# Feed-forward tile rebuilt: grid rounding through an integer Square in PSUM, new engines and orders for its steps

## The chip, the cores and the metric

The kernel runs on one core of a Trainium2 chip. The metric is the device time in microseconds (us) of one execution. Five queues run beside each other: TensorE (PE in the profile), VectorE (DVE), ScalarE (ACT), GpSimd (POOL) and SyncE (SP), which issues the transfers. They hand work to each other by counting semaphores.

## The reference

Input `x` is (16, 256, 256), `ctx` has the same shape. The first half is cross attention with 16 heads of 16; the second, which the change is about, is a feed-forward block whose three products are taken on blockwise FP4 values: each block of 16 values is scaled by its largest magnitude over 6, rounded to the grid 0, 0.5, 1, 1.5, 2, 3, 4, 6 with its sign, and scaled back.

```python
def fp4_quant_dequant(x):                 # BLOCK = 16
    scale = jnp.maximum(jnp.max(jnp.abs(xb), axis=-1, keepdims=True) / 6.0, 1e-12)
    xn = xb / scale
    q = _GRID[jnp.searchsorted(_MID, jnp.abs(xn))] * jnp.sign(xn) * scale
...
def _L0_ffn_ref(x, w_gate, w_up, w_down):   # 256 -> 704 -> 256
    gate = fp4_linear(x, w_gate)
    y = fp4_linear(x, w_up)
    h = jax.nn.silu(gate) * y
    return fp4_linear(h, w_down)
x = x + _L0_xattn_ref(_layernorm(x, axis=-1), ctx_1024, ctx_1024)
x = x + _L0_ffn_ref(_layernorm(x, axis=-1), w_gate, w_up, w_down)
```

## The kernel before

The attention runs first, as 16 pipelined steps of one batch each. Beside it the weights are rounded, a sixteenth a step. In the last full attention step (batch 15) TensorE transposes the rounded weights in 14 lots and VectorE copies each lot from PSUM to SBUF (`weights_out`). Then comes the feed-forward stage: 32 tiles of 128 rows. Nothing schedules it: each engine runs the function `ffn_step(st)` for step numbers that rise by one, and in step s an engine works on several tiles at once (`st.has(2)` guards the work on tile s+2, `st.has(-1)` that on tile s-1). An engine takes its instructions in the order in which they are written there.

A tile goes through these stages, with the lines of the program:

- normalise: statistics on VectorE (L709, L717, L722), the power -0.5 on GpSimd (L425), subtract and multiply on VectorE (L698);
- quantise x (256 wide, the program's XN and XC): block maxima (L704), limits and reciprocal (L607, L608, L612), multiply by the inverse on VectorE (L725), |z| times 2^22 on ScalarE (L516), max with a constant on VectorE (L731), add and subtract of that on GpSimd (L407, L409), multiply by the scale (L420);
- two transposes on TensorE into PSUM (L922) and a copy out on ScalarE (L511);
- four products of 352 columns (L909), gate and up, for the halves a = 0 and a = 1; Silu on ScalarE (L490), product with the up half on VectorE (L681), into HN;
- quantise h (704 wide): block maxima (L735), limits and reciprocal (L607, L608, L612), multiply (L738), three ScalarE statements (L521, L499, L501), add and subtract on GpSimd (L407, L409), multiply by the scale on VectorE (L753);
- six transposes (L933), copy out (L506), six products of 256 columns (L942), residual sum on VectorE (L689), store (L316).

Every buffer of the stage lies in the storage of the attention's `KS` and `QS`, so the profile shows XN, XC, HN, HC and the rest under those names. In PSUM, the products have banks of their own: gate halves in MX0 and SC0, up halves in PV and SC1. The x transposes lie in MX1, the result in SC2.

The rounding rests on adding a large number and subtracting it again, with a number that grows with |z|, so that the step of the fp32 sum is the step of the grid:

```python
def grid(z, c, sem_, wait_sem, st, off):          # GpSimd; c = max(|z| * 2^22 + ..., ...)
    nc.gpsimd.tensor_tensor(z, z, c, ALU.add).then_inc(sem_, 1)
    pool.wait_ge(sem_, st.times(off, 2, 1))
    nc.gpsimd.tensor_tensor(z, z, c, ALU.subtract).then_inc(sem_, 1)
```

Of the kernel before, what the change touches and what calls it, by code (L numbers as in the profile page):

```python
# [4 lines left out]
fp32 = mybir.dt.float32  # L5
bf16 = mybir.dt.bfloat16
ALU = mybir.AluOpType
# [5 lines left out]
QT = S // 128  # L13
# [12 lines left out]
MAGIC, ONE, UP, TINY = 2.0 ** 22, 1 + 2.0 ** -21, 1 + 2.0 ** -23, 1e-12  # L26
WCOLS = 3 * NT * D
# [4 lines left out]
CONSTS = 8  # L32
# [50 lines left out]
def ffn_steps(eng, body):  # L83
    steps(eng, body, 0, 5, (TILES - 8) // 2, 2, TILES + 3, TILES)


def program(nc, x, ctx_in, wg_in, wu_in, wd_in, out):
# [6 lines left out]
    with es:  # L94
# [17 lines left out]
        below = sb("below", [128, 1])  # L112
# [9 lines left out]
        KS = [sb(f"KS{r}", [128, H, S], bf16) for r in range(RING)]  # L122
        QS = [sb(f"QS{r}", [128, H, S], bf16) for r in range(RING)]
# [14 lines left out]
        fstats, fmv = sb("fstats", [128, 6]), [sb(f"fmv{r}", [128, 2]) for r in range(2)]  # L138
        fve = [sb(f"fve{r}", [128, 1]) for r in range(2)]
        frstd = [sb(f"frstd{r}", [128, 1]) for r in range(2)]  # L140
        xmax, xscale, xinv = ([sb(f"{n}{r}", [128, D // BLK]) for r in range(2)] for n in ("xmax", "xscale", "xinv"))
        hmax, hscale, hinv = ([sb(f"{n}{r}", [128, FI // BLK]) for r in range(2)] for n in ("hmax", "hscale", "hinv"))

        def carve(stack, *widths):

            words, at, carved = stack[:, :, :].rearrange("p h t -> p (h t)").bitcast(fp32), 0, []
            for w in widths:
                carved.append(words[:, at:at + w])
                at += w
            return carved  # L150

        WTR = [carve(z, 2 * FI)[0].rearrange("p (k c) -> p k c", k=2) for z in (KS[0], QS[0])]
        WDT = carve(KS[1], NT * D)[0].rearrange("p (k c) -> p k c", c=D)
        XN0, XN1, XC0, XC1, XQ0, XQ1, XT0, XT1 = carve(QS[1], *[D] * 8)
        XN = [XN0, XN1]
        XC = [XC0, XC1]
        XQ = [XQ0, XQ1]
        XT = [z.rearrange("p (k c) -> p k c", k=2) for z in (XT0, XT1)]
        (HN0, HC0, SG0), (HN1, HC1, SG1) = (carve(z, FI, FI, FH) for z in (KS[2], QS[2]))
        HN = [HN0, HN1]  # L160
        HC = [HC0, HC1]
        SG = [SG0, SG1]
        (HQ0, HQ1, OB0), (HT0, HT1, OB1) = (carve(z, NT * 128, NT * 128, D) for z in (KS[3], QS[3]))
        HQ = [HQ0, HQ1]
        HT = [z.rearrange("p (k c) -> p k c", k=NT) for z in (HT0, HT1)]
        OB = [OB0, OB1]

        SC = [pb(f"SC{r}", [128, QT, S]) for r in range(3)]
        MX = [pb(f"MX{r}", [128, QT, S]) for r in range(2)]
# [34 lines left out]
        h_abs, x_abs = sem("h_abs"), sem("x_abs")  # L204
        f_seq, fve_ready, frstd_ready = sem("f_seq"), sem("fve_ready"), sem("frstd_ready")
        x_seq, xc_ready, x_pool, xq_ready = sem("x_seq"), sem("xc_ready"), sem("x_pool"), sem("xq_ready")
        xp_ready, xt_ready, gu_ready, silu_done, h_done = (sem(n) for n in
            ("xp_ready", "xt_ready", "gu_ready", "silu_done", "h_done"))
        h_seq, hc_ready, h_pool, hq_ready = sem("h_seq"), sem("hc_ready"), sem("h_pool"), sem("hq_ready")
        hp_ready, ht_ready, down_ready, out_ready = (sem(n) for n in ("hp_ready", "ht_ready", "down_ready", "out_ready"))  # L210
# [29 lines left out]
        for m in range(2):  # L240
            for k in range(2):
                for a in range(2):
                    rs = range(3 * a, 3 * a + 3)
                    lots.append((WTR[m][:, k, 384 * a:min(FI, 384 * a + 384)],
                                 [WN[m][0:min(128, FI - 128 * r), r, 128 * k:128 * (k + 1)] for r in rs]))
        for c in range(NT):
            lots.append((WDT[:, c, :], [WD[:, r, 128 * c:128 * (c + 1)] for r in range(2)]))
# [9 lines left out]
        def _(sp):  # L257
# [62 lines left out]

            for t in (-3, -2):
                ffn_step(Step(t, TILES, 2))
            attention_step(Step(B - 1, B, RING))
            ffn_step(Step(-1, TILES, 2))
# [6 lines left out]
        def _(pool):  # L331
# [13 lines left out]
            nc.gpsimd.memset(below[:, :], -MAGIC * ONE).then_inc(consts, 1)  # L345

# [57 lines left out]
            def grid(z, c, sem_, wait_sem, st, off):  # L404

                pool.wait_ge(wait_sem, st.times(off, 1, 1))
                nc.gpsimd.tensor_tensor(z, z, c, ALU.add).then_inc(sem_, 1)  # L407
                pool.wait_ge(sem_, st.times(off, 2, 1))
                nc.gpsimd.tensor_tensor(z, z, c, ALU.subtract).then_inc(sem_, 1)  # L409

# [18 lines left out]
            for t in (-3, -2):  # L429
                ffn_step(Step(t, TILES, 2))  # L430
# [546 lines left out]
```

## Time and profile before

| | |
|---|---|
| time, median of 3 runs (lowest to highest) | 636.11 us (634.38 to 636.55) |
| the profiled execution: its time, its span | 636.03 us, 634.2 us |
| TensorE busy | 561.2 us, 88% of the span |
| VectorE busy | 515.0 us, 81% |
| ScalarE busy | 355.3 us, 56% |
| GpSimd busy | 324.4 us, 51% |
| attention with the weights | up to about 306 us of the span |
| first feed-forward product, last residual sum | 314.04 us, 631.55 us |

The span is that of the instructions; the rest of an execution's time, 1.8 us here, lies around it. Busy time is the union of an engine's instructions. The chain that ended last puts 41% of the span on TensorE and 25% on GpSimd, but it joins two stages that differ; the feed-forward stage has to be read by itself. The granted clock of TensorE over the span is 0.989 of full speed.

### The profile page before, as it was taken

The numbers are of one execution on the slowest core, as the hardware profiler recorded it, in microseconds if no ns is written. First come the engines' busy times: TensorE is split into PE (matmuls) and PEld (weight loads), VectorE is DVE, ScalarE is ACT, GpSimd is POOL, SyncE is SP. The second block draws the span as 40 slices with busy tenths as digits, with TensorE's granted clock in tenths as the row PEclk, the third lists the DMA queues.
The fourth block names the chain that finished last, engine by engine and source line by source line (L and its number), as shares of the span: only waits on it lengthen the run. The fifth ranks groups of instructions, "written<-read, shape, count | busy, mean of one in ns | idle before, by whom it ended". The sixth has DMA issues, their size and how long they took to land.

```text
span 634.2 us, 12943 instructions
## 1 busy us (share of the span) xinstructions
PE 561.2 (88%) x3561; PEld 341.6 (54%) x3588; DVE 515.0 (81%) x1171; ACT 355.3 (56%) x656; POOL 324.4 (51%) x386
## 2 busy tenths in 40 slices
PE   2489999999999999998679999999999999999996
PEld 1135555555555555545446665665665665665664
DVE  1498888889888888875478989889889889889863
ACT  2226877778877778776434445445345354354341
POOL 3243344444444444322356676776766766766740
PEclk9999999999999999999898999999999999999997
DMA  7834444444444443300000000000000000000000
GB/s 228 194 101 135 133 138 127 126 127 125 125 125 133 133 133 100 100 4 3 0 1 9 9 18 17 8 17 17 8 17 17 8 17 17 8 17 14 11 18 25
DMA packets 43796, 40.59 MB, mean 64 GB/s; under 512 B 4728, under 2 KB 43512, under 8 KB 43768
## 3 DMA queue, kind: packets, MB, share of 16 engines
q1 hardware_dynamic: 43768, 40.26, 22.4%
q8 instruction: 13, 0.21, 0.1%
q14 instruction: 15, 0.12, 0.1%
HBM read 10.55 MB, written 4.19 MB: 23 GB/s over the span
## 4 chain that ended last, share of the span: by engine, by line
PE 41%; POOL 25%; issue 15%; DVE 8%; ACT 5%; DMA 2%; SPq 2%; POOLq 1%; another core or an unknown queue 0%; ACTq 0%; DVEq 0%
PE PV L862 11%; PE SC L830 10%; PE MX L844 8%; POOL QS L409 6%; POOL QS L407 6%; POOL frstd L425 4%; POOL KS L409 4%; POOL KS L407 3%; PE T L772 3%; PE T L816 2%; PE SC L942 2%; ACT KP L448 2%; PE T L779 2%; POOL QS L420 2%; ACT P L457 1%
## 5 line engine op out<-in xcount | busy, mean ns | idle before, releaser
L544 DVE TENSOR_REDUCE MF<-MX 128x2 f32<-128x512 f32 x256 | 170.1, 686 | 32.8 <-PE MX L844 30.4
L457 ACT ACTIVATE P<-SC 128x512 f32<-128x512 f32 x256 | 147.2, 599 | 47.6 <-PE SC L830 45.7
L844 PE MATMUL MX<-KS,QS 96*128 96x256 bf16 x512 | 104.8, 289 | 6.9 <-DMA QS<-QP 3.4
L942 PE MATMUL SC<-KS,QS 128*128 128x256 f32 x384 | 93.8, 395 | 17.2 <-ACT QS L506 17.2
L830 PE MATMUL SC<-QS,KS 98*128 98x256 bf16 x512 | 99.7, 278 | 1.1 <-ACT P L457 0.7
L942 PEld LDWEIGHTS SC<-KS,QS 128*128 128x128 f32 x384 | 72.0, 194 | 42.6 <-ACT QS L506 33.7
L862 PE MATMUL PV<-P,VA 128*32 128x256 f32 x1024 | 81.6, 391 | 3.6
L407 POOL TENSOR_TENSOR QS<-QS 128x256 f32<-128x256 f32 (+1 forms) x47 | 48.3, 1027 | 63.9 <-ACT QS L501 35.8
L830 PEld LDWEIGHTS SC<-QS,KS 98*128 98x128 bf16 x512 | 39.2, 98 | 58.8 <-ACT P L457 31.9
L844 PEld LDWEIGHTS MX<-KS,QS 96*128 96x128 bf16 x512 | 47.6, 101 | 28.8 <-DVE MF L544 18.4
L409 POOL TENSOR_TENSOR QS<-QS 128x256 f32<-128x256 f32 (+1 forms) x47 | 49.8, 1059 | 3.7
L725 DVE TENSOR_TENSOR QS<-QS,xinv 128x256 f32<-128x256 f32 x32 | 51.2, 1600 | 0.0
L521 ACT ACTIVATE QS<-QS 128x704 f32<-128x704 f32 x16 | 12.7, 791 | 65.9 <-DVE QS L738 65.9
L521 ACT ACTIVATE KS<-KS 128x704 f32<-128x704 f32 x16 | 12.7, 791 | 64.7 <-DVE KS L738 64.7
L407 POOL TENSOR_TENSOR KS<-KS 128x704 f32<-128x704 f32 x16 | 26.9, 1680 | 40.9 <-ACT KS L501 40.9
L391 POOL TENSOR_TENSOR W<-W,WC 128x288 f32<-128x288 f32 (+1 forms) x16 | 12.7, 791 | 67.3 <-DVE WC L635 67.3
L909 PE MATMUL MX<-KS,QS 128*128 128x352 f32 x128 | 44.4, 470 | 1.0 <-ACT QS L511 1.0
L909 PE MATMUL SC<-KS,QS 128*128 128x352 f32 x128 | 44.4, 470 | 0.0
L909 PE MATMUL PV<-QS 128*128 128x352 f32 x128 | 43.2, 460 | 0.0
L909 PE MATMUL SC<-QS 128*128 128x352 f32 x128 | 43.2, 460 | 0.0
L425 POOL TENSOR_TENSOR frstd<-fve,mhalf 128x1 f32<-128x1 f32 x32 | 35.7, 1116 | 7.6 <-DVE fve L722 7.6
L448 ACT ACTIVATE KP<-T 128x512 bf16<-128x512 f32 x48 | 28.6, 596 | 18.4 <-PE T L772 12.2
(107 smaller groups left out, 993.4 us busy)
## 6 DMA issues: line engine op xcount, KB each, us to landing
KS<-KP SPq DMA_DIRECT2D x96, 128.0 KB, 2.4
QS<-QP SPq DMA_DIRECT2D x96, 128.0 KB, 2.4
X<-in_x SPq DMA_DIRECT2D x16, 256.0 KB, 2.9
C<-in_ctx SPq DMA_DIRECT2D x16, 256.0 KB, 3.1
out<-KS SPq DMA_DIRECT2D x16, 128.0 KB, 1.7
out<-QS SPq DMA_DIRECT2D x16, 128.0 KB, 1.7
W<-in_L_ffn_w_down SPq DMA_DIRECT2D x1, 704.0 KB, 8.3
W<-in_L_ffn_w_gate SPq DMA_DIRECT2D x1, 640.0 KB, 5.1
```

Source lines behind the costliest of these rows:

```text
L407: nc.gpsimd.tensor_tensor(z, z, c, ALU.add).then_inc(sem_, 1)
L409: nc.gpsimd.tensor_tensor(z, z, c, ALU.subtract).then_inc(sem_, 1)
L425: nc.gpsimd.tensor_tensor(frstd[r][:, :], fve[r][:, :], mhalf[:, 0:1], ALU.pow).then_inc(frstd_ready, 1)
L448: nc.scalar.activation(parts[:, n, :], bank, ACT.Copy).then_inc(out_sem, 1)
L457: nc.scalar.activation(P[g % 2][:, j, :, :], SC[h % 3][:, :, :], ACT.Exp, scale=0.25).then_inc(exp_done, 1)
L544: nc.vector.tensor_reduce(MF[st.slot(off, 2)][:, :, h:h + 1], MX[h % 2][:, :, :], AX.X, ALU.max, negate=True).then_inc(mx_done, 1)
L725: nc.vector.tensor_tensor(blocks(XN[r][:, :]), blocks(XN[r][:, :]), each(xinv[r][:, :]), ALU.mult).then_inc(x_seq, 1)
L830: last = nc.tensor.matmul(SC[h % 3][:, k, :], KS[r][0:ROWS, h, k * 128:(k + 1) * 128], QS[r][0:ROWS, h, :], start=True, stop=True)
L844: last = nc.tensor.matmul(MX[h % 2][:, q, :], QS[r][0:PROD, h, q * 128:(q + 1) * 128], KS[r][0:PROD, h, :], start=True, stop=True)
L862: last = nc.tensor.matmul(PV[32 * j:32 * (j + 1), g % 2, :], VA[r][:, k, HG * g + j, :], P[g % 2][:, j, k, :], start=(k == 0), stop=(k == ...
L909: last = nc.tensor.matmul((GP, UPP)[m][a], XT[st.slot(0, 2)][:, k, :], WTR[m][:, k, a * FH:(a + 1) * FH], start=(k == 0), stop=(k == 1))
L942: last = nc.tensor.matmul(DP, HT[r][:, c, :], WDT[:, c, :], start=(c == 0), stop=(c == NT - 1))
```

## The change

The steps of a feed-forward tile are redistributed and reordered. What stays: the tiles, the products with their sizes and operand types, the attention.

1. The grid. ScalarE squares the scaled z and writes the square as an integer into PSUM (one statement each for x and h); VectorE then adds the square, a constant and z, and in a second statement takes the square and constant minus z, which leaves the rounded value with its sign turned (the scales are negative now). ScalarE's Abs, Relu and Copy of h, its Abs of x, VectorE's max for x and GpSimd's four add and subtract statements go.
2. No VectorE statement reads two tensors from SBUF. The multiplications by the inverses and by the h scale, which had two SBUF inputs on VectorE (L725, L738, L753), are on GpSimd; normalising is one ScalarE Identity with a bias and a scale; the block maxima and the statistics lie in PSUM, so the limits read PSUM.
3. PSUM: one gate bank G and one up bank U serve both halves, so each product waits for the reader of the one before.
4. The order of each engine's work in a step; x is prepared one tile further ahead (`st.has(4)`); two steps instead of one and two of the ramp stand before the last attention step, and two behind it.
5. `weights_out` is on ScalarE.
6. `XN`, `XQ`, `OB` and `SG` have SBUF of their own; h buffers and weights lie in `KS` and `QS` still, at other places. GpSimd's power is taken over two columns.

```diff
-        GP = [MX[0][:, :, :].rearrange("p q s -> p (q s)")[:, 0:FH], SC[0][:, :, :].rearrange("p q s -> p (q s)")[:, 0:FH]]
-        UPP = [PV[:, :, :].rearrange("p q s -> p (q s)")[:, 0:FH], SC[1][:, :, :].rearrange("p q s -> p (q s)")[:, 0:FH]]
-        DP = SC[2][:, 0, :]
-        XP = MX[1][:, 0, :].rearrange("p (k c) -> p k c", k=2)
+        G = bank(SC[0])[:, 0:FH]
+        U = bank(SC[1])[:, 0:FH]
+        hmax = bank(SC[1])[:, FH:FH + FI // BLK]
+        XP = bank(SC[2])[:, 0:D]
+        DP = PV[:, 0, :]
+        fmv, xmax = PV[:, 1, 0:2], PV[:, 1, 16:16 + D // BLK]
+        SQ = MXB[:, :, :, :].rearrange("p r q s -> p (r q s)").bitcast(int32)
+        HSQ, XSQ = SQ[:, 0:FI], SQ[:, FI:FI + D]
...
@@ GpSimd, ffn_step
-                if st.has(-1) and st.first < TILES:
-                    grid(HN[r][:, :], HC[r][:, :], h_pool, hc_ready, st, -1)
-                if st.has(2):
-                    grid(XN[r][:, :], XC[r][:, :], x_pool, xc_ready, st, 2)
...
+                if st.has(-1):
+                    pool.wait_ge(h_inv, st.times(-1, 1, 1))
+                    nc.gpsimd.tensor_tensor(blocks(HN[r][:, :]), blocks(HN[r][:, :]), each(hinv[r][:, :]),
+                                            ALU.mult).then_inc(hm_ready, 1)
+                if st.has(4):
+                    nc.gpsimd.tensor_tensor(frstd[r][:, :], fve[r][:, :], mhalf[:, :], ALU.pow).then_inc(frstd_ready, 1)
+                if st.has(-1):
+                    pool.wait_ge(h_grid, st.times(-1, 1, 1))
+                    nc.gpsimd.tensor_tensor(blocks(HQ[r][:, 0:FI]), blocks(HN[r][:, :]), each(hscale[r][:, :]),
+                                            ALU.mult).then_inc(hq_ready, 1)
...
@@ ScalarE, ffn_step
+                if st.has(3):
+                    nc.scalar.activation(XN[r][:, :], tile(st.item(3)), ACT.Identity, bias=fbias[r][:, 0:1],
+                                         scale=frstd[r][:, 0:1]).then_inc(xn_ready, 1)
                 if st.has(0):
                     silu(st, 0)
+                if st.has(-1):
+                    act.wait_ge(hm_ready, st.times(-1, 1, 1))
+                    if st.has(1):
+                        act.wait_ge(x_grid, st.times(1, 1, 1))
+                    nc.scalar.activation(HSQ, HN[r][:, :], ACT.Square, scale=CURVE).then_inc(hsq_ready, 1)
...
@@ VectorE
+            def round_up(z, square, done):
+                nc.vector.scalar_tensor_tensor(z, square, BASE, z, ALU.add, ALU.add).then_inc(done, 1)
+
+            def round_back(z, square, done):
+                nc.vector.scalar_tensor_tensor(z, square, BASE, z, ALU.add, ALU.subtract).then_inc(done, 1)
...
@@ TensorE, inner(st, a, m) and the down product
+                    pe.wait_ge(silu_done, st.times(0, 2, a))
+                elif a == 0:
+                    pe.wait_ge(h_lim, st.times(-1, 2, 2))
+                else:
+                    pe.wait_ge(h_done, st.times(0, 2, 1))
...
+                    product(DP, HH[r], WDH, NT).then_inc(down_ready, 1)
```

On TensorE, the two steps of the loop stood like this; T is the PSUM of the h transposes, the rows of L909 are the gate and up products, L922 the x transposes, L942 the down product.

```order
L909 MATMUL MX<-KS,QS 128x352 x2
L909 MATMUL PV<-QS 128x352 x2
L919 REGISTER_ALU
L922 MATMUL MX<-ident,QS 128x128 x2
L907 REGISTER_ALU
L909 MATMUL SC<-KS,QS 128x352 x2
L928 REGISTER_ALU
L931 REGISTER_ALU
L933 MATMUL T<-ident,KS 128x128 x6
L909 MATMUL SC<-QS 128x352 x2
L942 MATMUL SC<-KS,QS 128x256 x6
```

The same step of the changed kernel; L934 holds all products, L953 both kinds of transposes.

```order
L953 MATMUL T<-ident,HQ 128x128 x6
L942 REGISTER_ALU
L943 ISA
L934 MATMUL SC<-WH,XH 128x352 x2
L971 REGISTER_ALU
L953 MATMUL SC<-ident,XQ 128x128 x2
L934 MATMUL SC<-WH,XH 128x352 x2
L943 REGISTER_ALU
L934 MATMUL SC<-WH,XH 128x352 x4
L988 REGISTER_ALU
L934 MATMUL PV<-WDH,HH 128x256 x6
```

The number and size of the matmuls are the same; the h transposes moved from between the second half's two products to the head of the step, and the x transposes one product forward.

On VectorE, the second part of a step, from the up product's multiplication (L681) on:

```order
L725 TENSOR_TENSOR QS<-QS,xinv 128x256
L681 TENSOR_TENSOR KS<-SC,QS 128x352
L731 TENSOR_SCALAR QS<-QS 128x256
L735 TENSOR_REDUCE hmax<-KS 128x44
L607 TENSOR_SCALAR hscale<-hmax 128x44
L608 TENSOR_SCALAR hinv<-hmax 128x44
L612 RECIPROCAL hinv<-hinv 128x44
L738 TENSOR_TENSOR KS<-KS,hinv 128x704
L753 TENSOR_TENSOR KS<-QS,hscale 128x704
```

And of the changed kernel, from the first half's multiplication (L702) to the end of the step:

```order
L702 TENSOR_TENSOR HN<-SC,SG 128x352
L718 SCALAR_TENSOR_TENSOR HN<-MX,HN 128x704
L762 RECIPROCAL xinv<-xinv 128x16
L721 SCALAR_TENSOR_TENSOR HN<-MX,HN 128x704
L702 TENSOR_TENSOR HN<-SC,SG 128x352
L770 TENSOR_REDUCE SC<-HN 128x44
L718 SCALAR_TENSOR_TENSOR XN<-MX,XN 128x256
L721 SCALAR_TENSOR_TENSOR XN<-MX,XN 128x256
L714 TENSOR_SCALAR hscale<-SC 128x44
L715 TENSOR_SCALAR hinv<-SC 128x44
L783 RECIPROCAL hinv<-hinv 128x44
```

The two rounding statements of the previous tile's h now stand between the two halves of this tile, the two of x stand between the h maxima and the h limits, and the multiplications with block values are gone from the engine.

## Rows read from the trace of the kernel before

**Rows 1.** Busy time by engine, from the page.
```profile
PE 561.2 (88%) x3561; PEld 341.6 (54%) x3588; DVE 515.0 (81%) x1171; ACT 355.3 (56%) x656; POOL 324.4 (51%) x386
```

**Rows 2.** Stretches of the feed-forward stage: length, busy PE, PEld, DVE, ACT, POOL, granted clock.
```profile
310.00:360.00 50.00, 40.41 (x151) 27.20 (x152) 37.38 (x89) 18.67 (x36) 32.21 (x34) 0.93 0.02 6
360.00:410.00 50.00, 46.17 (x187) 30.11 (x186) 45.20 (x100) 22.22 (x40) 34.92 (x34) 1.00 0.04 14
```

**Rows 3.** Timeline, TensorE, one tile: start, length, what, idle before it.
```profile
449.98 0.88 PE L933 MATMUL T<-ident,KS 128*128 128x128 f32 x6
450.69 1.35 PE L909 MATMUL SC<-QS 128*128 128x352 f32 x4
452.63 2.86 PE L942 MATMUL SC<-KS,QS 128*128 128x256 f32 x12 [0.60 <-ACT QS L506]
455.33 1.35 PE L909 MATMUL MX<-KS,QS 128*128 128x352 f32 x4
456.51 1.35 PE L909 MATMUL PV<-QS 128*128 128x352 f32 x4
458.05 0.44 PE L922 MATMUL MX<-ident,QS 128*128 128x128 f32 x2 [0.19 <-POOL QS L420]
458.32 1.35 PE L909 MATMUL SC<-KS,QS 128*128 128x352 f32 x4
459.68 0.87 PE L933 MATMUL T<-ident,KS 128*128 128x128 f32 x6
```

**Rows 4.** Timeline of the same tile, the other engines.
```profile
451.96 1.67 POOL L407 TENSOR_TENSOR QS<-QS 128x704 f32<-128x704 f32 x1 [2.44 <-ACT QS L501]
452.08 1.84 DVE L725 TENSOR_TENSOR QS<-QS,xinv 128x256 f32<-128x256 f32 x1
453.71 1.75 POOL L409 TENSOR_TENSOR QS<-QS 128x704 f32<-128x704 f32 x1
453.95 0.42 ACT L516 ACTIVATE QS<-QS 128x256 f32<-128x256 f32 x1 [1.09 <-DVE QS L725]
454.75 0.53 DVE L681 TENSOR_TENSOR KS<-SC,QS 128x352 f32<-128x352 f32 x1 [0.83 <-ACT QS L490]
455.54 0.87 DVE L735 TENSOR_REDUCE hmax<-KS 128x44 f32<-128x704 f32 x1
456.54 0.72 DVE L608 TENSOR_SCALAR hinv<-hmax 128x44 f32<-128x44 f32 x1
457.75 0.99 DVE L738 TENSOR_TENSOR KS<-KS,hinv 128x704 f32<-128x704 f32 x1
458.77 0.79 ACT L521 ACTIVATE KS<-KS 128x704 f32<-128x704 f32 x1 [4.06 <-DVE KS L738]
461.58 1.67 POOL L407 TENSOR_TENSOR KS<-KS 128x704 f32<-128x704 f32 x1 [2.44 <-ACT KS L501]
```

**Rows 5.** Timeline, ramp: end of the attention, first product.
```profile
292.68 0.42 ACT L516 ACTIVATE QS<-QS 128x256 f32<-128x256 f32 x1 [2.51 <-DVE QS L725]
...
314.04 2.56 PE L909 MATMUL MX<-KS,QS 128*128 128x352 f32 x4
```

**Rows 6.** Timeline of the last tiles.
```profile
596.14 0.42 DVE L725 TENSOR_TENSOR QS<-QS,xinv 128x256 f32<-128x256 f32 x1
...
609.27 1.35 PE L909 MATMUL MX<-KS,QS 128*128 128x352 f32 x4
609.29 0.17 DVE L608 TENSOR_SCALAR hinv<-hmax 128x44 f32<-128x44 f32 x1
...
621.29 5.49 PE L942 MATMUL SC<-KS,QS 128*128 128x256 f32 x12 [0.90 <-ACT QS L506]
...
631.55 0.42 DVE L689 TENSOR_TENSOR QS<-SC,X 128x256 f32<-128x256 f32 x1 [4.31 <-PE SC L942]
```

**Rows 7.** GpSimd groups by shape: busy us, mean ns, idle before.
```profile
L407 POOL TENSOR_TENSOR QS<-QS 128x256 f32<-128x256 f32 x32 | 23.2, 726 | 28.1 <-DVE QS L731 28.1
L397 POOL TENSOR_TENSOR W<-W,wscale 128x288 f32<-128x288 f32 x8 | 5.4, 676 | 1.4 <-POOL W L394 1.4
```

More of the change, by code:

```diff
@@ L344, in _ @@
                                         base=0, pattern=[[-1, 128]], channel_multiplier=1).then_inc(consts, 1)
-            nc.gpsimd.memset(below[:, :], -MAGIC * ONE).then_inc(consts, 1)
+            for r in range(2):
+                nc.gpsimd.memset(fve[r][:, :], 1.0).then_inc(consts, 1)
             nc.gpsimd.memset(mhalf[:, :], -0.5).then_inc(consts, 1)
@@ L489, in silu @@
                 act.wait_ge(h_done, st.times(-1, 2, a + 1))
-                nc.scalar.activation(SG[a][:, :], GP[a], ACT.Silu).then_inc(silu_done, 1)
+                nc.scalar.activation(SG[a][:, :], G, ACT.Silu).then_inc(silu_done, 1)
             def ffn_step(st):
-                if st.has(0):
-                    silu(st, 0)
-                if st.has(-1) and st.first < TILES:
-                    r = st.slot(-1, 2)
-                    act.wait_ge(h_abs, st.times(-1, 2, 1))
-                    nc.scalar.activation(HC[r][:, :], HC[r][:, :], ACT.Relu, bias=below[:, :]).then_inc(h_abs, 1)
-                    act.wait_ge(h_abs, st.times(-1, 2, 2))
-                    nc.scalar.activation(HC[r][:, :], HC[r][:, :], ACT.Copy, bias=MAGIC * ONE).then_inc(hc_ready, 1)
                 if st.has(-2):
@@ L612, in invert @@
                 nc.vector.reciprocal(inv, inv).then_inc(sem_, 1)
-            def scales(amax, scale, inv, sem_, per, first, st, off):
-                limits(amax, scale, inv, sem_, per, first, st, off)
-                invert(inv, sem_, per, first, st, off)
-                dve.wait_ge(sem_, st.times(off, per, first + 3))
             def weight_maxima(st):
@@ new lines, in round_up @@
+            def round_up(z, square, done):
+                nc.vector.scalar_tensor_tensor(z, square, BASE, z, ALU.add, ALU.add).then_inc(done, 1)
+            def round_back(z, square, done):
+                nc.vector.scalar_tensor_tensor(z, square, BASE, z, ALU.add, ALU.subtract).then_inc(done, 1)
+            def ffn_step(st):
+                mean_var, amax = (fmv0[:, :], xmax0[:, :]) if st.first < 0 else (fmv, xmax)
+                if st.first == 0:
+                    dve.wait_ge(pv_out, 2 * B)
+                if st.has(4):
+                    dve.wait_ge(x1_ready, st.times(4, 1, 1))
+                    gate(dve)
+                    nc.vector.bn_stats(fstats[:, :], tile(st.item(4))).then_inc(f_stats, 1)
@@ L749, in ffn_step @@
[L749 to L754 removed]
+                    dve.wait_ge(h_max, st.times(0, 1, 1))
+                    block_limits(hmax, hscale[r][:, :], hinv[r][:, :], h_lim)
@@ L900, in attention_step, with product @@
                             values(st, g, 1)
+            def product(dst, x, w, count):
+                for c in range(count):
+                    last = nc.tensor.matmul(dst, x[:, c, :], w[:, c, :], start=(c == 0), stop=(c == count - 1))
+                return last
             def inner(st, a, m):
+                r = st.slot(0, 2)
                 if m == 0:
@@ L930, in ffn_step @@
                         pe.wait_ge(zeroed, 2)
+                        pe.wait_ge(o_norm, QT * B)
                     pe.wait_ge(ht_ready, st.times(-2, 1))
                     for c in range(NT):
-                        last = nc.tensor.transpose(HP[:, c, :], HQ[r][:, 128 * c:128 * (c + 1)], ident[:, :])
+                        last = turn(HP[:, c, :], HQ[r][:, 128 * c:128 * (c + 1)], c % 4 == 0)
                     last.then_inc(hp_ready, 1)
+                if st.has(0):
+                    inner(st, 0, 0)
+                if st.has(1):
+                    r = st.slot(1, 2)
+                    pe.wait_ge(xq_ready, st.times(1, 1, 1))
+                    pe.wait_ge(xt_ready, st.times(1, 1))
+                    if st.first == -1:
+                        pe.wait_ge(exp_done, B * H)
+                    for k in range(2):
+                        last = turn(XP[:, 128 * k:128 * (k + 1)], XQ[r][:, 128 * k:128 * (k + 1)], k == 0)
+                    last.then_inc(xp_ready, 1)
+                if st.has(0):
+                    inner(st, 0, 1)
+                    inner(st, 1, 0)
                 if st.has(0):
@@ L940, in ffn_step @@
                     pe.wait_ge(out_ready, st.times(-2, 1))
-                    for c in range(NT):
-                        last = nc.tensor.matmul(DP, HT[r][:, c, :], WDT[:, c, :], start=(c == 0), stop=(c == NT - 1))
-                    last.then_inc(down_ready, 1)
+                    if st.has(4):
+                        pe.wait_ge(fneg_ready, st.times(4, 1, 1))
+                    elif st.has(3):
+                        pe.wait_ge(x_lim, st.times(3, 2, 2))
+                    product(DP, HH[r], WDH, NT).then_inc(down_ready, 1)
             pe.wait_ge(consts, CONSTS)
```

289 lines of the change are left out of this document (146 added, 143 removed).

## The prediction

> **What bounds the kernel now.** The page's busy times come first [rows 1]: TensorE 88% and VectorE 81% of the span, no other engine above 56%. These are means over two unlike stages, and the change touches only the second, so the next view is that of stretches. From 360 to 410 us, a steady piece of the feed-forward stage, TensorE is busy 46.2 of 50 us and VectorE 45.2 [rows 2]. Both look nearly full, and the question is which of them sets the pace.
>
> The timeline of one tile answers it. TensorE first [rows 3]. I take what a group costs as the distance to the start of the next group where that did not wait: six h transposes 0.71 us (449.98 to 450.69), four products of the gate and up kind 1.18 each (455.33 to 456.51), the down product 2.70 (452.63 to 455.33), two x transposes 0.27. The sum is 0.71 + 4.72 + 2.70 + 0.27 = 8.40 us. But the tile takes 9.62 us: GpSimd's L407 starts at 451.96 and again, one tile on, at 461.58 [rows 4]. So TensorE loses 1.2 us a tile, part as idle time before the down product (0.60, for ScalarE's copy) and before the x transposes (0.19), the rest where a group has to drain before the next may start.
>
> The other engines show the ring that sets 9.62 [rows 4]. GpSimd's L407 starts at 451.96. VectorE's L725, a multiplication with two inputs in SBUF, starts at 452.08 and takes 1.84 us; at 596.14, with no GpSimd statement beside its start, the same statement takes 0.42 [rows 6]. It ends 0.29 us after GpSimd's L407 does: it was held. Behind it come ScalarE's L516 (453.95), a Silu, the second up half (L681, 454.75), the h maxima (L735, 455.54), the limits, of which L608 takes 0.72 here and 0.17 at 609.29 [rows 4, 6], the multiplication L738 (457.75 to 458.74), and three ScalarE statements from 458.77 on, which release GpSimd's next L407. The two holds add 1.42 + 0.55 = 2.0 us to VectorE's tile. L681 (one input in PSUM) took 0.53 us although GpSimd's L409 ran beside it from 453.71 to 455.46 [rows 4], so such a statement is not held.
>
> **The change, part by part.** The sum is made against the profiled execution, 636.03 us; the median of the runs, 636.11, is the same within 0.1.
>
> TensorE keeps its groups, so 8.40 us a tile is its floor. The reordering puts h transposes, whose input is a whole step old, directly behind the down product, and the x transposes between two products; nothing then has to drain. The single gate and up banks add waits: the second gate product waits for the first Silu, which has 1.45 us for it (the up product and x transposes between, 1.18 + 0.27) and needs about 0.5 for the 352 elements that L681 takes 0.53 for; the second up product waits for VectorE's first half, 0.53 us [rows 4], behind a gate product of 1.18. Both fit. If a queue is late there, up to 0.4 us a tile comes back. I take 8.45 us a tile.
>
> VectorE's new list per tile, by the nearest rows: rounding of h twice. The operation, two tensors and a constant with the square in PSUM, has no row. Its lower bound is one pass at the pace of the maxima, 0.87 for 704 elements; its upper bound twice that, 1.74. I take 0.89, because L681 with a PSUM and an SBUF input costs 0.53 for 352, and the statement reads no more than that does. Rounding of x twice at 0.42 each, two halves 1.06, h maxima 0.87, x maxima, statistics and residual sum at 0.42 each, limits and reciprocals together about 1.3 with the small ones: some 7.5 us, below 8.45. The list before was longer by the three block multiplications and the holds.
>
> GpSimd: two block multiplications of 704. L397 costs 676 ns for 288 against 726 ns for a plain 256 [rows 7]. Plain 704 costs 1.67 [rows 4], so the slope is (1.67 - 0.73)/448 = 2.1 ns per element; with it, 704 costs 0.68 + 416 x 2.1 ns = 1.55, with L397's own mean per element 1.65, and if its fixed part is like the plain one's, 1.4. I take 1.5. With two of 256 for x (0.6 each) and the power this is about 5.3 us a tile, not the bound; and GpSimd's four add and subtract statements go. ScalarE goes down to seven statements, the two largest 0.79 like L521 [rows 4], some 3.6 us: cover for each is an engine idle more than half of the tile. A write of integers to PSUM has no row; between nothing and twice 0.79 it adds at most 0.8 to the ring below.
>
> The new ring runs through h: second half 0.53, h maxima 0.87, the two x roundings that stand behind them 0.84, limits and reciprocal 0.79 (455.54 + 0.87 to 457.75, less the hold of 0.55), GpSimd 1.5, Square 0.79, the two h roundings 1.78, and then the next tile's second half, which stands behind them in VectorE's queue. With nine handovers at 0.03 to 0.05 (L725 to L516 took 0.03) that is 7.1 + 0.4 = 7.5 us. TensorE sets the pace with 0.9 us to spare.
>
> Stage by stage. From the first product of tile 0 (314.04) to that of tile 31 (609.27) the kernel now takes 295.2 us [rows 5, 6]. After: 31 x 8.45 = 262, plus 2 for half clock in the ramp (0.93 granted from 310 to 360 us is some 7 us at 1.2 instead of 2.4 GHz [rows 2]; before, other waits hid part of that), so 264: a gain of 31.2. The two first tiles lack transposes and down products, and wait for their chain instead; I let these cancel. Tail: now 631.97 - 609.27 = 22.7. After: four products 4.9, then 0.53 + 0.87 + 0.79 + 1.5 + 0.79 + 1.78, GpSimd 1.5, transposes 0.88, copy 0.79, down product 2.86, residual 0.42, handovers 0.4, together 18.0; the idle gaps let the clock fall as now, where the down product took 5.49 instead of 2.86 [rows 6, 3], so plus 3: 21.0, a gain of 1.7.
>
> The passage from attention costs nothing net in my sum. The wait of ScalarE for VectorE inside the last attention step, 2.5 us at 292.68 [rows 5], goes, and a shorter one for the first tile's bias comes. Against it, ScalarE gets 14 weight copies, about 0.42 each by its 256-wide statement [rows 4], 5.9 us beside the exponentials of one step; TensorE's next lot and VectorE wait for them. And the last batch's evacuation now stands behind the preparation of tiles 1 and 2 on ScalarE, with GpSimd's sums of the last two batches queued behind three feed-forward multiplications. The first product would come at 314 again, give or take 3.
>
> 636.0 - 31.2 - 1.7 = 603.1; I forecast 603.
>
> **Rivals.** First, the ring through h takes over: handovers or GpSimd's multiplications dearer than taken, or the square slower into PSUM. With 1.0 to 1.5 us more the tile takes 8.6 to 9.0, and the time is 603 + 31 x (0.15 to 0.55) = 608 to 620. For it: the ring has seven steps on three engines, of which three have no row. Against it: 0.9 us of slack. Chance 0.24.
>
> Second, slower than before: the rounding statements run at half pace, 1.74 and 0.84. That adds 2.6 to the ring, 7.5 + 2.6 = 10.1, and to VectorE's list, 10.1 as well; the starts that overlap take back 0.3. 31 x (9.8 - 8.45) = 42, so about 645. It decides from a rounding cost of 1.7 us for 704 elements on, where the tile takes the present 9.5. Against it: L681 and its full pace [rows 4]. Chance 0.06.
>
> The Trainium skill ("Vector Engine (DVE) Microarchitecture Reference", "Points that are easy to get wrong") says that a scalar_tensor_tensor with two SBUF sources wider than bf16 halves its throughput. One of the two lies in PSUM here, so by the letter of the rule the sum stays; if it held here nevertheless, it would be this rival. No row of this trace shows the operation.
>
> Third, the change does not do what it says: VectorE is still held by GpSimd, by 1.4 us a tile or more, and the tile stays at 9.5: 636. L681 speaks against it. Chance 0.02. Mishaps of the ramp make up the rest.
>
> **How the numbers follow.** TensorE's pace as forecast 0.67 (598 to 608); the h ring 0.24 (608 to 620); slower 0.06; no change 0.03. The range takes in the first case and most of the second: 596, the ramp 3 us better and no clock lost in the tail, to 617. A difference under 0.3%, 2 us, is about what a measurement of this kernel can't tell from none. Faster 0.91, same 0.03, slower 0.06.
>
> **What would show it.** Right: distance between equal TensorE groups 8.4 to 8.5 us; TensorE busy all of a steady stretch; L718 and L721 at 0.9 for 704 elements; no VectorE statement stretched beside GpSimd; idle time on VectorE before the first half. Wrong: idle time on TensorE before L934 put down to VectorE; L718 at 1.7; a first product later than 317 us.

## The result and the profile after

The changed kernel takes 593.13 us (median of 4, 591.61 to 593.94) where the kernel before took 635.25 in the runs beside it: 0.933 of it, with a 95% interval of 0.9305 to 0.9362. The forecast was 603 us with a range of 596 to 617. The direction, the mechanism and the new bound were forecast; the gain was put at 33 us and is 42, and the time lies outside the range.

From the page of the changed kernel: busy time by engine, and how the chain of work that ended last divides over the engines.

```profile
PE 541.5 (92%) x3561; PEld 346.9 (59%) x3588; DVE 447.8 (76%) x1154; ACT 329.9 (56%) x640; POOL 269.6 (46%) x389
PE 80%; issue 5%; ACT 5%; DVE 3%; POOL 2%; DMA 2%; SPq 2%; another core or an unknown queue 0%; POOLq 0%; ACTq 0%; DVEq 0%
```

Stretches of the same stage as in [rows 2] (length, busy PE, PEld, DVE, ACT, POOL, granted clock):

```profile
310.00:360.00 50.00, 44.87 (x189) 30.72 (x182) 36.24 (x113) 20.57 (x41) 28.13 (x40) 0.91 0.03 9
360.00:410.00 50.00, 50.00 (x220) 37.09 (x220) 41.04 (x117) 21.20 (x43) 28.56 (x36) 1.00 0.05 16
```

TensorE is busy for all 50 us of the steady stretch, where it had 46.17, and VectorE went from 45.20 to 41.04. TensorE's timeline for one tile, to be held against [rows 3]:

```profile
445.60 0.82 PE L953 MATMUL T<-ident,HQ 128*128 128x128 f32 x6
446.25 1.35 PE L934 MATMUL SC<-WH,XH 128*128 128x352 f32 x4
447.44 0.38 PE L953 MATMUL SC<-ident,XQ 128*128 128x128 f32 x2
447.66 3.72 PE L934 MATMUL SC<-WH,XH 128*128 128x352 f32 x12
451.21 2.75 PE L934 MATMUL PV<-WDH,HH 128*128 128x256 f32 x12
453.80 0.82 PE L953 MATMUL T<-ident,HQ 128*128 128x128 f32 x6
```

No group waited. From start to start: h transposes 0.65, gate product 1.19, x transposes 0.22, three products 3.55, down product 2.59, together 8.20 us a tile instead of 9.62. That is 0.25 under the 8.45 of the forecast, and 0.2 under what the forecast called TensorE's floor. The other engines from a tile's first half (L702) on, to be held against [rows 4]; L422 ends this tile's rounding, L411 and L535 begin the next one's:

```profile
441.04 0.53 DVE L702 TENSOR_TENSOR HN<-SC,SG 128x352 f32<-128x352 f32 x1 [0.29 <-PE SC L934]
441.48 0.88 DVE L718 SCALAR_TENSOR_TENSOR HN<-MX,HN 128x704 f32<-128x704 int32 x1
442.43 0.85 DVE L721 SCALAR_TENSOR_TENSOR HN<-MX,HN 128x704 f32<-128x704 int32 x1
443.44 1.39 POOL L422 TENSOR_TENSOR HQ<-HN,hscale 128x704 f32<-128x704 f32 x1 [2.13 <-DVE HN L721]
446.42 1.39 POOL L411 TENSOR_TENSOR HN<-HN,hinv 128x704 f32<-128x704 f32 x1
448.08 0.76 ACT L535 ACTIVATE MX<-HN 128x704 int32<-128x704 f32 x1
```

The operations that had no row cost what the forecast took or less: the rounding statements 0.88 and 0.85 us (0.89 taken), the Square into PSUM 0.76 (0.79), GpSimd's block multiplication 1.39 (1.5). VectorE now waits for TensorE before the first half (0.29).

Ramp and tail, TensorE's and VectorE's rows that answer to [rows 5, 6]:

```profile
309.18 0.66 PE L953 MATMUL SC<-ident,XQ 128*128 128x128 f32 x2 [3.59 <-POOL XQ L433]
309.77 1.94 PE L892 MATMUL PV<-P,VA 128*32 128x256 f32 x16
315.39 2.55 PE L934 MATMUL SC<-WH,XH 128*128 128x352 f32 x4
...
569.28 4.90 PE L934 MATMUL SC<-WH,XH 128*128 128x352 f32 x16
...
584.07 4.54 PE L934 MATMUL PV<-WDH,HH 128*128 128x256 f32 x12 [0.90 <-ACT HH L520]
588.65 0.42 DVE L710 TENSOR_TENSOR OB<-PV,X 128x256 f32<-128x256 f32 x1 [7.00 <-PE PV L934]
```

They divide the gain of the spans, 634.2 - 591.3 = 42.9 us, into the parts of the forecast:

| part | before | after | gain | forecast gain |
|---|---|---|---|---|
| to tile 0's first product | 314.0 | 315.4 | -1.4 | 0 |
| from there to tile 31's first product | 295.2 | 253.9 | 41.3 | 31.2 |
| from there to the end of the last residual sum | 22.7 | 19.8 | 2.9 | 1.7 |

### The profile page after: what moved, and what is told of

Same layout as the page of the kernel before. It is cut to its first block, busy times and chain, and to the rows that moved or that the text cites. A ratio compares the mean times of both kernels' runs of the same rounds, so it can differ in the third digit from the quotient of the medians.

```text
span 591.3 us, 12747 instructions
## 1 busy us (share of the span) xinstructions
PE 541.5 (92%) x3561; PEld 346.9 (59%) x3588; DVE 447.8 (76%) x1154; ACT 329.9 (56%) x640; POOL 269.6 (46%) x389
## 4 chain that ended last, share of the span: by engine, by line
PE 80%; issue 5%; ACT 5%; DVE 3%; POOL 2%; DMA 2%; SPq 2%; another core or an unknown queue 0%; POOLq 0%; ACTq 0%; DVEq 0%
PE SC L934 24%; PE PV L934 13%; PE PV L892 12%; PE SC L860 10%; PE MX L874 9%; PE T L953 4%; PE T L802 3%; PE T L846 3%; ACT P L473 2%; ACT KP L464 2%; PE T L809 2%; DVE MF L576 2%; PE SC L953 1%; DMA QS<-QP 1%; SPq L274 1%
## 5 line engine op out<-in xcount | busy, mean ns | idle before, releaser
L934 PE MATMUL SC<-WH,XH 128*128 128x352 f32 x512 | 163.2, 463 | 0.0
L934 PEld LDWEIGHTS SC<-WH,XH 128*128 128x128 f32 x512 | 93.2, 192 | 41.4 <-DVE HN L702 3.6
L874 PE MATMUL MX<-KS,QS 96*128 96x256 bf16 x512 | 104.4, 288 | 8.6 <-DMA QS<-QP 4.2
L934 PE MATMUL PV<-WDH,HH 128*128 128x256 f32 x384 | 90.0, 385 | 1.8 <-ACT HH L520 1.8
L934 PEld LDWEIGHTS PV<-WDH,HH 128*128 128x128 f32 x384 | 74.0, 193 | 17.2 <-ACT HH L520 2.3
L422 POOL TENSOR_TENSOR HQ<-HN,hscale 128x704 f32<-128x704 f32 x32 | 44.4, 1387 | 77.0 <-DVE HN L721 77.0
L520 ACT ACTIVATE HH<-T 128x768 f32<-128x768 f32 x32 | 25.9, 810 | 92.7 <-PE T L953 92.7
L874 PEld LDWEIGHTS MX<-KS,QS 96*128 96x128 bf16 x512 | 47.4, 100 | 30.4 <-DVE MF L576 18.6
L513 ACT ACTIVATE SG<-SC 128x352 f32<-128x352 f32 x64 | 29.4, 459 | 41.5 <-PE SC L934 41.5
L702 DVE TENSOR_TENSOR HN<-SC,SG 128x352 f32<-128x352 f32 x64 | 33.6, 525 | 22.5 <-PE SC L934 20.8
L411 POOL TENSOR_TENSOR HN<-HN,hinv 128x704 f32<-128x704 f32 x32 | 44.4, 1386 | 2.1 <-DVE hinv L783 2.0
L464 ACT ACTIVATE QP<-T 128x512 bf16<-128x512 f32 x48 | 29.2, 608 | 14.7 <-PE T L809 8.3
```

Of the source, the lines that this page charges most:

```text
L411: nc.gpsimd.tensor_tensor(blocks(HN[r][:, :]), blocks(HN[r][:, :]), each(hinv[r][:, :]), ALU.mult).then_inc(hm_ready, 1)
L422: nc.gpsimd.tensor_tensor(blocks(HQ[r][:, 0:FI]), blocks(HN[r][:, :]), each(hscale[r][:, :]), ALU.mult).then_inc(hq_ready, 1)
L464: nc.scalar.activation(parts[:, n, :], bank, ACT.Copy).then_inc(out_sem, 1)
L513: nc.scalar.activation(SG[a][:, :], G, ACT.Silu).then_inc(silu_done, 1)
L702: nc.vector.tensor_tensor(HN[st.slot(0, 2)][:, a * FH:(a + 1) * FH], U, SG[a][:, :], ALU.mult).then_inc(h_done, 1)
L874: last = nc.tensor.matmul(MX[h % 2][:, q, :], QS[r][0:PROD, h, q * 128:(q + 1) * 128], KS[r][0:PROD, h, :], start=True, stop=True)
```

## The experiments

The theory at this point, called A: TensorE alone sets the tile's 8.20 us; the ring through h needs 7.3 to 7.5; a statement of VectorE with two SBUF inputs is held by one of GpSimd that is running; and the 0.2 us a tile by which TensorE's floor was read too high is what a group costs more when it had to wait and could not load its first weights ahead. Its rivals: the ring is close behind TensorE (B), the hold has another cause, or TensorE's groups got cheaper by their new buffers. Most kernels here ran once; their times are compared with the 593.1 of the changed kernel and the 635.9 to 636.4 of the kernel before in the same sets of runs, and most verdicts rest on rows.

Two parts of a run move by themselves, and a single time has to be read with that in mind. The first is the start: early products of the attention wait for a transfer (L874; L875 in the kernel with the extra statement). In the changed kernel, in the one with the extra PSUM statement and in the one with the weight copies on VectorE:

```profile
27.43 0.61 PE L874 MATMUL MX<-KS,QS 96*128 96x256 bf16 x2 [4.21 <-DMA QS<-QP]
29.10 0.61 PE L875 MATMUL MX<-KS,QS 96*128 96x256 bf16 x2 [5.42 <-DMA QS<-QP]
30.09 0.61 PE L874 MATMUL MX<-KS,QS 96*128 96x256 bf16 x2 [5.65 <-DMA QS<-QP]
```

No edit touches this stretch, and it differs by up to 2.7 us. The second is the last down product: 4.54 us in the trace of the changed kernel, 2.86 in that of the kernel with the weight copies on VectorE, whose tail is the same. That is 1.7 us of granted clock which no edit there explains.

**Less work on TensorE.** One and three of the six down products left out:

```diff
-                    product(DP, HH[r], WDH, NT).then_inc(down_ready, 1)
+                    product(DP, HH[r], WDH, 5).then_inc(down_ready, 1)
```

(3 in the second kernel.)

> The changed kernel with one of the six products of each down projection left out (the result lacks that part of the sum). Theory A, TensorE alone sets the tile's 8.20 us and the ring through h needs about 7.4: one product pair costs 2.59/6 = 0.43 us, so the tile takes 7.77 and the time falls by 31 x 0.43 = 13 us to about 580. Theory B, the ring through h (VectorE's roundings, GpSimd, Square) is within 0.2 us of TensorE: the tile stays at 8.0 or more and the time at 587 or more.

> The changed kernel with three of the six products of each down projection left out. TensorE alone would need 8.20 - 1.30 = 6.90 us a tile and the time would be about 553. Theory A, with the ring through h at 7.3 to 7.5 us: the tile takes that, VectorE has no idle time ahead of the first half and GpSimd's multiplication releases Square late; time 565 to 571. Theory B: 8.0 or more, 587.

Measured: 579.5 us with five, 13.6 less, so the product pair (31 x 0.43 = 13.3) comes through whole. With three, 573.0: far from 553, but also 2.0 us above A's 565 to 571, of which the later start (28.72 against 27.43) explains 1.3. Steady rows with three:

```profile
443.52 1.39 POOL L422 TENSOR_TENSOR HQ<-HN,hscale 128x704 f32<-128x704 f32 x1 [2.16 <-DVE HN L721]
445.04 0.87 PE L953 MATMUL T<-ident,HQ 128*128 128x128 f32 x6 [0.46 <-POOL HQ L422]
441.56 0.88 DVE L718 SCALAR_TENSOR_TENSOR HN<-MX,HN 128x704 f32<-128x704 int32 x1
449.17 0.88 DVE L718 SCALAR_TENSOR_TENSOR HN<-MX,HN 128x704 f32<-128x704 int32 x1
```

The tile takes 7.61 us (441.56 to 449.17), a little over A's 7.3 to 7.5, and TensorE waits 0.46 us for GpSimd's HQ. So B is out: there were 0.6 us of slack behind TensorE. But the next ring is not the one that I had written down. As I read the rows, it runs rounding, GpSimd's multiplication by the scale, h transposes, the tile's first two products with the x transposes between them, and VectorE's first half, which stands ahead of the next rounding.

**One more statement on VectorE**, once with an input in PSUM, once with both in SBUF, ahead of the h maxima:

```diff
+                    nc.vector.tensor_tensor(C[0][:, 0, :], U[:, 0:D], HN[r][:, D:2 * D], ALU.add)
```

```diff
+                    nc.vector.tensor_tensor(C[0][:, 0, :], HN[r][:, 0:D], HN[r][:, D:2 * D], ALU.add)
```

> The changed kernel with one more VectorE statement per tile, 256 elements, one input in PSUM and one in SBUF, just before the h maxima, while GpSimd's multiplication by the h scale runs. Both theories: 0.42 us on VectorE, not held. Theory A (0.8 us of slack in the ring): time unchanged within 1 us. Theory B: 0.2 to 0.4 us a tile more, 6 to 12 us.

> The same extra statement with both inputs in SBUF. If a VectorE statement with two SBUF inputs is held by a GpSimd statement that runs, it starts at about 443.8 beside GpSimd's 1.39 us statement and takes 1.2 to 1.4 us instead of 0.42; the ring then needs 8.2 to 8.6 us and the time rises by 0 to 12 us. If the hold seen before had another cause (the block inverse read 16 times over, for one), it takes 0.42 and the time is that of the run with one PSUM input.

Measured: 595.1 and 601.1 us. The first is 2 us over the changed kernel where A allowed 1; 1.7 of them lie in the start (29.10 against 27.43), and the tile stays at 8.20 us. In the second the tile takes 8.44 us on average (316.35 to 578.12 for 31). Rows of the kernel with the PSUM input, then of the one with two SBUF inputs:

```profile
445.38 1.39 POOL L422 TENSOR_TENSOR HQ<-HN,hscale 128x704 f32<-128x704 f32 x1 [2.13 <-DVE HN L721]
445.79 0.42 DVE L770 TENSOR_TENSOR C<-SC,HN 128x256 f32<-128x256 f32 x1
```

```profile
439.92 1.39 POOL L422 TENSOR_TENSOR HQ<-HN,hscale 128x704 f32<-128x704 f32 x1 [1.90 <-DVE HN L721]
440.27 1.32 DVE L770 TENSOR_TENSOR C<-HN 128x256 f32<-128x256 f32 x1
441.26 0.81 POOL L427 TENSOR_TENSOR XN<-XN,xinv 128x256 f32<-128x256 f32 x1
```

The same work at the same place takes 0.42 us or 1.32, and in the second case it ends at 441.59, 0.28 after GpSimd's statement does at 441.31; the hold of L725 before looked the same. GpSimd's next statement in turn takes 0.81 us instead of 0.62. The statement reads nothing 16 times over, so that is not the cause. The Trainium skill ("SBUF — State Buffer", "SBUF: two separate sides") describes this as a pair of SBUF ports that the two engines share, which a VectorE statement with two SBUF inputs and a GpSimd statement cannot hold together and which whoever starts first keeps; the rows agree.

**The h multiplication by the inverse on VectorE again**, the statement of before with its two SBUF inputs:

```diff
-                    nc.gpsimd.tensor_tensor(blocks(HN[r][:, :]), blocks(HN[r][:, :]), each(hinv[r][:, :]),
-                                            ALU.mult).then_inc(hm_ready, 1)
...
+                    dve.wait_ge(h_inv, st.times(0, 1, 1))
+                    nc.vector.tensor_tensor(blocks(HN[r][:, :]), blocks(HN[r][:, :]), each(hinv[r][:, :]),
+                                            ALU.mult).then_inc(hm_ready, 1)
```

> The changed kernel with the h multiplication by the inverse on VectorE again (704 elements, two inputs in SBUF) instead of GpSimd. Theory A: VectorE's 7.3 us busy of 8.2 become 8.2 to 8.5 with the hold by GpSimd's statement for x that runs just then, so VectorE takes over from TensorE: 8.3 to 8.7 us a tile, time 596 to 609, and the statement takes 1.0 to 1.3 us. Rival: where the multiplication stands does not matter, because the order and the rounding made the gain: 8.2 us, 592 to 595.

Measured: 592.7 us. My expectation failed, in its price as in its sum:

```profile
445.81 0.89 DVE L780 TENSOR_TENSOR HN<-HN,hinv 128x704 f32<-128x704 f32 x1
445.83 0.92 POOL L434 TENSOR_TENSOR fbias<-fneg,frstd 128x1 f32<-128x1 f32 x1
360.00:410.00 50.00, 50.00 (x221) 37.17 (x220) 46.09 (x122) 21.48 (x43) 24.91 (x30) 1.00 0.05 16
```

VectorE started 0.02 us ahead of GpSimd, so GpSimd was held: its one-column product took 0.92 us instead of the 0.19 of the changed kernel. VectorE is busy 46.1 of 50 us and TensorE all of them. That no VectorE statement has two SBUF inputs is therefore no condition of the gain; only what else runs when one starts matters. The kernel before had this hold in both directions too: its one-column power (L425) takes 1.20 us in the steady tiles, where VectorE's L738 has started just before it, and 0.55 at 311.37, where no such statement runs.

**All three block multiplications on VectorE**, as before the change (the edit above, and the same for the h scale behind L721 and for x behind that):

> The changed kernel with all three block multiplications that the kernel before had on VectorE there again: h by its inverse, h by its scale, x by its inverse. Theory A: VectorE, busy 46.1 of 50 us with the first of them back, gets 0.89 + 0.42 us more a tile and becomes the bound: 8.9 us of work and what GpSimd's x statement and the ring add, 8.9 to 9.4 us a tile, time 615 to 631. Rival: what the change gained is the order and the rounding; with TensorE still the bound 8.2 to 8.4, 593 to 600.

Measured: 617.2 us. Two rows of VectorE, one tile apart:

```profile
439.90 0.52 DVE L686 TENSOR_TENSOR HN<-SC,SG 128x352 f32<-128x352 f32 x1
449.04 0.52 DVE L686 TENSOR_TENSOR HN<-SC,SG 128x352 f32<-128x352 f32 x1
```

9.14 us a tile, in the middle of what A gave. With the rest of the change in place, moving the three multiplications is worth 24 of the 42 us by the times, and 26 of the 41 by the stretch between the first products of tiles 0 and 31 (280.2 us here, 253.9 in the changed kernel). The other 15 to 18 come from the rest taken together (rounding and orders), which was not divided further. Since the first of the three costs nothing on VectorE by itself, this is no sum of three separate parts.

**The down product without its wait, in the kernel before:**

```diff
-                    pe.wait_ge(ht_ready, st.times(-2, 1, 1))
...
-                        last = nc.tensor.matmul(DP, HT[r][:, c, :], WDT[:, c, :], start=(c == 0), stop=(c == NT - 1))
+                        last = nc.tensor.matmul(DP, WDT[:, c, 0:128], WDT[:, c, :], start=(c == 0), stop=(c == NT - 1))
```

> The kernel before, with the down product's stationary operand read from a fixed slice of the weights, so that TensorE waits for no copy ahead of that group (the result is not the block's). Theory A: TensorE was not in the ring that set 9.62 us, so the idle 0.60 us ahead of the group goes elsewhere and the tile stays at 9.62, time 634 to 637; and a group whose first weights can be loaded while the group before still runs costs less from start to start than the 2.70 us read from a group that had waited: 2.59, with the start record 0.1 us behind the weight load. Rival: TensorE was in the ring and the tile falls by 0.3 to 0.6 us, time 618 to 627; or the group keeps 2.70, and the lower cost in the changed kernel comes from its banks and buffers.

Measured: 631.7 us. Rows of TensorE and GpSimd:

```profile
439.18 1.20 POOL L425 TENSOR_TENSOR frstd<-fve,mhalf 128x1 f32<-128x1 f32 x1
442.50 2.64 PEld L941 LDWEIGHTS SC<-KS 128*128 128x128 f32 x12
442.79 2.75 PE L941 MATMUL SC<-KS 128*128 128x256 f32 x12
445.38 1.35 PE L909 MATMUL MX<-KS,QS 128*128 128x352 f32 x4
448.81 1.20 POOL L425 TENSOR_TENSOR frstd<-fve,mhalf 128x1 f32<-128x1 f32 x1
```

The tile stays at 9.63 us (439.18 to 448.81): TensorE was not in the ring of before. And the group costs 2.59 (442.79 to 445.38) in the old banks and buffers, as in the changed kernel; its weight load starts 0.29 us ahead of its first matmul, where the load and matmul of the waiting group start together. The 4 us that it is faster lie in the last tiles, where the wait for the copy was exposed. 2.7 of them are clock: the down product that took 5.49 us takes 2.76 there. Whether the edit did that is not shown, as the clock of such a group differs between kernels with the same tail, too.

**The h transposes back in their old place** on TensorE, between the two products of the second half, with ScalarE's copy behind that of x:

> The changed kernel with the h transposes back between the two products of the second half on TensorE, and their copy on ScalarE behind that of the x transposes. Theory A: TensorE lost time before only where it really waited, and here nothing waits there: HQ is old, the copy ends 0.3 us before the down product: 8.20 us a tile, 592 to 595. Rival: the place of the transposes is what took the drains away: 0.3 to 0.6 us a tile more, 602 to 612.

Measured: 594.3 us, within A's 592 to 595, but not by A's 8.20 us a tile:

```profile
436.07 2.85 PE L934 MATMUL PV<-WDH,HH 128*128 128x256 f32 x12
...
443.46 0.81 ACT L540 ACTIVATE HH<-T 128x768 f32<-128x768 f32 x1 [1.54 <-PE T L953]
444.39 2.46 PEld L934 LDWEIGHTS PV<-WDH,HH 128*128 128x128 f32 x12 [0.43 <-issue]
444.40 2.85 PE L934 MATMUL PV<-WDH,HH 128*128 128x256 f32 x12
447.09 1.35 PE L934 MATMUL SC<-WH,XH 128*128 128x352 f32 x4
```

The tile takes 8.33 us (436.07 to 444.40). The copy ends at 444.27, 0.13 us before the down product starts, so TensorE shows no idle time. Yet its weight load starts only with the group, not 0.29 us ahead, and the group costs 2.69 again. An operand that is just in time was too late here for the early weight load. The place of the transposes is no matter of 0.3 to 0.6 us a tile, as the rival had it, but of 0.13. The time hides part of that, because the last down product ran at full clock (2.86 us).

**The weight copies on VectorE again:**

> The changed kernel with the 14 weight copies of the last attention step on VectorE again. Theory A: the copies were no bound on either engine: TensorE's last attention scores come at 304 to 305 as before, the first product within 1 us of 315.4, time 592 to 594. Rival: on ScalarE they delayed the exponentials and with them the end of the attention, so the first product comes 1 to 3 us sooner here, time 590 to 592.

Measured: 594.6 us, and the first product comes at 317.94 instead of 315.39, so neither expectation holds as it stands. But the whole delay lies in the start: it is there at 30.09 against 27.43. From there to TensorE's last attention products ahead of the passage it is 277.6 us (to 307.66), in the changed kernel 277.5 (to 304.95). So it makes no difference to the attention which engine copies the weights, as A had it.

**The order of the passage.** The last batch's final step ahead of ramp step -1, on every engine; and in a second kernel ahead of both ramp steps:

```diff
             attention_step(Step(B - 1, B, RING))
-            for t in (-2, -1):
-                ffn_step(Step(t, TILES, 2))
+            ffn_step(Step(-2, TILES, 2))
             attention_step(Step(B, B, RING))
+            ffn_step(Step(-1, TILES, 2))
```

> The changed kernel with the last batch's final step of the attention ahead of ramp step -1 instead of behind it, on all engines. The trace of the changed kernel has TensorE idle for 3.59 us at 305.6, waiting for the x of tile 0 with the last attention products queued behind it, and then at half clock. Theory A: those products run at 305.6, the first product of tile 0 comes at 312 to 314 instead of 315.4, and the time falls by 1 to 3 us. Rival: the preparation of tiles 1 and 2 is what the ramp waits for, and it comes as much later: time unchanged within 1 us.

> The changed kernel with the last batch's final step ahead of both ramp steps -2 and -1. Theory A: GpSimd's sums of the last two batches no longer stand behind feed-forward statements, the first product comes at 311 to 313, and the time falls by 2 to 4 us. Rival: x of tiles 0 and 1 comes 1.5 us later on ScalarE and VectorE, so that the ramp loses there what it gains: unchanged within 1 us, or 1 to 2 us slower.

Measured: 591.0 us, ratio to before 0.9303 (0.9278 to 0.9327), and 594.0, 0.9338 (0.9315 to 0.9361). Neither interval is clear of that of the changed kernel (0.9305 to 0.9362), so rows must tell. The first product of tile 0 comes at 312.72 in the one kernel and at 316.20 in the other:

```profile
306.69 1.07 PE L892 MATMUL PV<-P,VA 128*32 128x256 f32 x16 [0.39 <-ACT P L473]
312.72 2.63 PE L934 MATMUL SC<-WH,XH 128*128 128x352 f32 x4 [0.47 <-ACT XH L540]
316.44 1.28 ACT L513 ACT_TABLE_LOAD   x1
318.25 3.82 PE L934 MATMUL SC<-WH,XH 128*128 128x352 f32 x12 [1.04 <-ACT SG L513]
```

```profile
315.07 0.66 PE L953 MATMUL SC<-ident,XQ 128*128 128x128 f32 x2 [3.80 <-issue]
316.20 2.72 PE L934 MATMUL SC<-WH,XH 128*128 128x352 f32 x4 [0.47 <-ACT XH L540]
```

For the first product the theory holds in the first kernel, 2.7 us sooner, and the rival in the second: there VectorE starts to round the x of tile 0 only behind its work for the last batch, at 313.41 instead of 307.52. But the first kernel loses 1.5 of its 2.7 us again before tile 31 (255.4 us from first product to first product, not 253.9). 1.04 of them are a wait for Silu behind a table load of ScalarE, which lay ahead of the first product in the changed kernel, at 313.53. So the rows leave this order some 1.2 us, and another 1.7 us of the profiled execution's gain is the clock of the last down product (2.86).

**Combined:** the first of these two orders, the h multiplication by the inverse on VectorE, and the multiplication by the scale on VectorE for the last tile alone.

> Three edits of the changed kernel together: the last batch's final step ahead of ramp step -1; the h multiplication by the inverse on VectorE; and the last tile's multiplication by the scale on VectorE, which is idle there. Each shortens the chain of the ramp or the tail, none touches TensorE's 8.2 us: 2 us from the first as measured, 0.5 us for each tile of the tail's chain from the second (0.89 against 1.39 us) and 0.5 from the third: 589 to 590.5. Rival: VectorE at 92% busy with the h multiplication makes the ramp later: 592 or more.

Measured: 590.08 us (5 runs, 589.39 to 590.72), ratio to before 0.927 (0.925 to 0.929), against 0.9305 to 0.9362 for the changed kernel: faster than both. The last tile:

```profile
581.16 0.87 PE L957 MATMUL T<-ident,HQ 128*128 128x128 f32 x6 [0.57 <-DVE HQ L765]
582.94 2.86 PE L938 MATMUL PV<-WDH,HH 128*128 128x256 f32 x12 [0.90 <-ACT HH L515]
```

The idle time before the transposes fell from 1.11 to 0.57 us, which is the third edit. The last down product ran at full clock, 2.86 instead of 4.54 us; as it does so in kernels with an unedited tail too, that this is the work of the edits is not shown. The second edit gave the tail nothing, against the expectation: with it alone the tail takes the 19.8 us of the changed kernel.

## Why the prediction missed

**Right.** What bound the kernel before (the ring with VectorE's two holds, not TensorE); that it would go and TensorE take its place; the prices of the three operations without a row; the waits that the single gate and up banks add, which never show; half clock at both ends in the profiled execution (0.91 granted from 310 to 360 us, 4.54 us for the last down product). The time is outside the range mainly because one term of the sum was too large.

**The step that failed** is "The sum is 0.71 + 4.72 + 2.70 + 0.27 = 8.40 us" and the sentence that this "is its floor". I took a group's cost from its start to the next group's where the next did not wait, but three of the four groups had themselves waited, and their start to start holds the load of their first weights. For the h transposes [rows 3] do not show it; their weight load does, which starts with them at 449.97 after 0.49 us of waiting for VectorE's L753. Without the wait they cost 0.65, 2.59 and 0.22: the floor is 8.20. The down product's share is shown by the kernel before without its wait and, the other way round, by the late transposes; for the two kinds of transposes it is read from the rows. With the 0.05 added for drains this is 31 x 0.25 = 7.8 us of the 10.1 by which the long part was overestimated. (VectorE's list was off too, without effect: its own terms add up to 7.1 us, not 7.5, and it is busy 6.7 of 8.20.)

**The other 2.3 us** of that part lie in the ramp, where the missing work of the first tiles was taken to cancel with their waits:

```profile
325.13 0.44 PE L953 MATMUL SC<-ident,XQ 128*128 128x128 f32 x2 [1.84 <-POOL XQ L433]
330.72 0.88 PE L953 MATMUL T<-ident,HQ 128*128 128x128 f32 x6 [1.60 <-POOL HQ L422]
331.43 1.35 PE L934 MATMUL SC<-WH,XH 128*128 128x352 f32 x4
```

From tile 0's first product to tile 2's it is 16.04 us (315.39 to 331.43), 0.36 less than two steady tiles. Two down products and one set of h transposes are missing there, 5.83 us, and TensorE waits 1.84 + 1.60 = 3.44. What is left, 2.0 us, is half clock with the drains, as forecast. So the step that failed here is "I let these cancel": the missing groups outweigh the waits by 2.4 us.

**The tail** gained 2.9 instead of 1.7 us. Its chain was forecast at 18.0 plus 3 for the clock and took 19.8: the last down product lost 1.7 us to the clock, not 3, and the rest took 18.1. That 1.7 is luck of the execution: seven kernels of the experiments lost nothing there, and three of them have the same tail (the weight copies and both orders of the passage). **The passage** lost 1.4 us where nothing was forecast, give or take 3. 0.5 of that is the start (27.43 against 26.89). The attention then got 1.0 us shorter (277.5 us from there to TensorE's last product group of eight, where it was 278.6), and what follows up to the first feed-forward product 1.85 longer (10.44 where it was 8.59): TensorE stood 3.59 us with the last attention products queued behind the x transposes, and ran them at half pace (1.94 us for a group that took 1.07). I had named the evacuation behind ScalarE's preparation, but not that wait on TensorE.

**Of the rivals**, half-pace rounding and VectorE held as before are refuted by rows. A ring through h sets the tile at 7.6 us once TensorE has less to do, so it was 0.6 us away, less than the 0.9 that I gave it.

## What to carry to other kernels

Read an engine's floor from groups that did not wait themselves: on TensorE, the distance from start to start of a group that had waited held its first weight load here, and a row whose weight load and matmul start together marks it. When an engine that is not the bound shows a stretched statement, look at what ran on the engine beside it, and by whose start it was decided, before all such statements are moved; one of the three moved here could have stayed. Before the time of a single run is credited to an edit, compare the stretches that the edit does not touch: here the start and the last group moved by 2.7 and 1.7 us. And in a passage between stages, look for the last work of the old stage queued behind the first wait of the new one.

## What the hardware showed that I had not expected

An operand that was ready 0.13 us before its group of matmuls started still cost that group its early weight load (2.69 against 2.59 us), with no idle time in the trace. The hold between VectorE and GpSimd works in both directions: a one-column product of GpSimd took 0.92 us instead of 0.19 when a VectorE statement with two SBUF inputs had started 0.02 us ahead. GpSimd's power took 1.20 us for one column in the steady tiles of the kernel before, beside VectorE's L738, and 0.55 without such a neighbour; for two columns it takes 0.69 in the changed kernel.
